# Twelve attention layers on one core: score matmuls that wait for one bank each, restacking by row slot, and softmax denominators spread by a VectorE shuffle

## What is computed

```python
for i in range(6):                                    # D=128, 16 heads of 8 channels, DFF=512
    xn = adaln(x, noise_emb, n1_w[i], n1_b[i])        # layernorm, gain and shift from the condition
    q, k, v = split(xn @ qkv_w[i].T); q, k = rope(q), rope(k)
    x = x + softmax(q k / sqrt(8)) v @ so_w[i].T      # over 512 tokens
    xn = adaln(x, noise_emb, n2_w[i], n2_b[i])
    q = rope(xn @ cq_w[i].T); k = rope(context @ ck_w[i].T); v = context @ cv_w[i].T
    x = x + softmax(q k / sqrt(8)) v @ co_w[i].T      # over 154 context tokens
    xn = adaln(x, noise_emb, n3_w[i], n3_b[i])
    x = x + gelu(xn @ f1_w[i].T + f1_b[i]) @ f2_w[i].T + f2_b[i]
```

## Time and profile before

| | |
|---|---|
| median of 3 runs | 3327.22 us (3326.3 to 3336.64) |
| the profiled execution's own time | 3326.18 us |
| its span, first to last instruction | 3324.4 us |
| mean granted TensorE clock | 0.956 |
| PE busy | 2934.0 us (88%) |
| DVE busy | 2097.4 us (63%) |
| ACT busy | 1917.6 us (58%) |
| POOL busy | 823.6 us (25%) |
| first stack, from about 720 to 1943 us | 6 layers |
| second stack, from about 2000 to 3213 us | 6 layers |

### The profile page before, as it was taken

One profiled execution on the slowest core, in us unless ns is written; L12 is line 12 of the kernel. 1 busy time (PEld: TensorE's weight loads), 2 busy tenths in 40 slices (PEclk: granted clock), 3 DMA queues, 4 the chain that ended last, 5 costly groups with the idle time before them and its releaser, 6 DMA issues.

```text
span 3324.4 us, 44923 instructions
## 1 busy us (share of the span) xinstructions
PE 2934.0 (88%) x15735; PEld 1036.8 (31%) x15735; DVE 2097.4 (63%) x3631; ACT 1917.6 (58%) x2693; POOL 823.6 (25%) x1327
## 2 busy tenths in 40 slices
PE   7998999977989899898989856989989898998978
PEld 2473333321222323222232222232322223232226
DVE  4316776637668495766848465848576684857634
ACT  5433333334758576675857642857667585766742
POOL 0002455431222222222222201222222222222211
PEclk9999999987999999999999976999999899999999
DMA  1101000001111111111111100111111111111130
GB/s 45 58 1 26 1 1 1 1 16 37 32 34 39 40 34 37 41 38 32 41 41 29 42 13 20 40 40 29 40 45 36 32 41 40 29 38 45 38 128 7
DMA packets 125514, 110.11 MB, mean 33 GB/s; under 512 B 49982, under 2 KB 116076, under 8 KB 125292
## 3 DMA queue, kind: packets, MB, share of 16 engines
q1 hardware_dynamic: 114924, 97.80, 9.9%
q10 hardware_dynamic: 10368, 9.44, 0.9%
HBM read 41.96 MB, written 0.52 MB: 13 GB/s over the span
## 4 chain that ended last, share of the span: by engine, by line
PE 65%; DVE 18%; ACT 6%; issue 4%; POOL 3%; SPq 1%; ACTq 1%; DMA 1%; DVEq 0%; POOLq 0%
PE ps L515 12%; DVE arena L798 7%; PE ps L460 7%; PE ps L489 3%; PE ps L588 3%; PE ps L631 3%; PE ps L646 3%; PE ps L532 3%; PE ps L574 2%; PE ps L1492 2%; PE ps L523 2%; PE ps L1480 2%; PE ps L544 2%; PE ps L563 2%; ACT arena L671 2%
## 5 line engine op out<-in xcount | busy, mean ns | idle before, releaser
L671 ACT ACTIVATE arena<-ps 128x1024 f32<-128x1024 f32 x960 | 934.4, 1022 | 245.9 <-PE ps L489 235.5
L798 DVE TENSOR_REDUCE arena<-ps 128x1 f32<-128x512 f32 x1536 | 964.6, 683 | 118.9 <-PE ps L460 109.7
L515 PE MATMUL ps<-arena 128*32 128x512 f32 x3840 | 504.2, 606 | 2.2 <-ACT arena L690 1.2
L460 PE MATMUL ps<-arena 49*128 49x512 bf16 x1536 | 311.6, 402 | 149.0 <-DVE arena L798 107.7
L800 DVE TENSOR_REDUCE arena<-ps 128x3 f32<-128x462 f32 (+1 forms) x576 | 305.2, 579 | 137.6 <-PE ps L467 116.3
L489 PE MATMUL ps<-arena 52*128 52x512 bf16 x1920 | 342.9, 385 | 29.5 <-ACT arena L671 8.6
L880 POOL TENSOR_TENSOR arena<-arena,zeros 128x16 bf16<-128x16 f32 x192 | 42.3, 220 | 1085.7 <-DVE arena L798 711.6
L460 PEld LDWEIGHTS ps<-arena 49*128 49x128 bf16 x1536 | 75.0, 93 | 542.9 <-DVE arena L798 470.8
L890 POOL TENSOR_TENSOR arena<-arena 128x512 f32<-128x512 f32 x96 | 122.1, 1272 | 387.4 <-ACT arena L703 384.1
L1552 ACT ACTIVATE arena<-ps 128x1024 f32<-128x1024 f32 x96 | 98.1, 1022 | 165.9 <-DVE ps L1639 128.9
L355 PE MATMUL ps<-consts 128*128 128x512 f32 x336 | 163.4, 612 | 23.7 <-DVE arena L2076 23.7
(11 more groups left out here) (383 smaller groups left out, 4366.5 us busy)
## 6 DMA issues: line engine op xcount, KB each, us to landing
arena<-arena SPq DMA_DIRECT2D x720, 64.0 KB
arena<-we_dram SPq DMA_DIRECT2D x24, 578.5 KB, 7.5
arena<-arena ACTq DMA_DIRECT2D x144, 64.0 KB
w<-weights_dram SPq DMA_DIRECT2D x26, 320.0 KB, 3.2
w<-weights_dram SPq DMA_DIRECT2D x13, 512.0 KB, 4.2
arena<-arena SPq DMA_DIRECT2D x384, 6.0 KB
arena<-arena SPq DMA_DIRECT2D x288, 19.2 KB
w<-weights_dram SPq DMA_DIRECT2D x39, 128.0 KB, 2.2
```

The lines of the kernel that those rows point to most:

```text
L460: pe.matmul(s_bank(slot + r), qst[b][rows, idx, P * qt:P * (qt + 1)], kst[b][rows, idx, :], start=True, stop=True).then_inc(s_full, 1)
L515: mm = pe.matmul(bank(7)[32 * j:32 * j + 32, :], v, prob[:, slot, j, :], start=(g % 2 == 0 and kt == 0), stop=(a == 0 and g % 2 == 1 and k ...
L671: act.activation(prob[:, chunk_no(b, a, g, kt) % NPROB, 2 * p:2 * p + 2, :], e_bank(slot).rearrange("p (j n) -> p j n", j=2), ACT.Exp, sca ...
L798: op = ve.tensor_reduce(nmax[:, g % 2, r, n:n + 1], s_bank(slot + r), AX.X, ALU.max, negate=True)
```

## The change

Four things change together.

1. **Score waits.** In self attention each of the two score matmuls waits for its own bank, not the first for both. Some waits of DVE and ACT are put in another sequence within one instruction.
2. **Restacking by row slot.** An `st` item is now one slot (two DMAs, four for the context's k) and waits for the part which that slot holds. The number of DMAs stays 96 a layer. Nine items, 18 DMAs a layer, are issued by ACT, where it was two items with 12 DMAs.
3. **Denominators.** The matmul in `sel` is gone, with `selector2` and what made it. DVE instead runs a `stream_shuffle` within each 32 partitions from `osb` to `rlog`, 8 a layer of 128 x 512 fp32; ACT's logarithm reads that from SBUF, and `sel` no longer uses a PSUM slot. The shuffle waits for `evac` and for the `inv` before it.
4. **Order.** `PLACES` has new numbers for all items (392 places, since `st` has more items), and `FILL` has 11 useless matmuls a layer in other places.

```diff
-PER_LAYER = 371
+PER_LAYER = 392
...
-        def restack(eng, b, u, part):
-            for slot in slots_of(u, part):
-                for r in range(2):
-                    rows = slice(64 * r + slot, 64 * r + ROW_MASK, PARTS)
...
+        def restack(eng, b, u, slot):
+            part = part_in(u, slot)
+            for r in range(2):
+                rows = slice(64 * r + slot, 64 * r + ROW_MASK, PARTS)
...
-        ACT_STACKS = (("st", 0, 1, 0), ("st", 1, 2, 0))
+        ACT_STACKS = (("st", 0, 1, 0), ("st", 0, 1, 1), ("st", 0, 2, 4), ("st", 1, 0, 2), ("st", 1, 0, 3),
+                      ("st", 1, 0, 5), ("st", 1, 1, 0), ("st", 1, 2, 4), ("st", 1, 2, 5))
...
-        FILL = {("out", 0, 1): 3, ("out", 1, 1): 2, ("f1", 0, 0): 1, ("score", 1, 1, 0, 0): 2, ("center", 0, 2): 1}
+        FILL = {('center', 0, 2): 1, ('out', 0, 1): 2, ('out', 1, 1): 3, ('score', 0, 0, 0, 4): 1, ('score',
+                0, 0, 1, 2): 1, ('score', 1, 1, 0, 0): 2, ('var', 0, 2): 1}
...
             def score(it):
...
-                pe.wait_ge(s_free, z.room("s", it, 2))
                 if a == 0:
                     idx, qt = 2 * g + n // 4, n % 4
                     for r in range(2):
                         rows = slice(64 * r, 64 * r + K_SCORE)
+                        pe.wait_ge(s_free, z.room("s", it, 1) if r == 0 else floor0(at - 1))
                         pe.matmul(s_bank(slot + r), qst[b][rows, idx, P * qt:P * (qt + 1)], kst[b][rows, idx, :],
                                  start=True, stop=True).then_inc(s_full, 1)
                     return
+                pe.wait_ge(s_free, z.room("s", it, 2))
...
-            def sel(it):
-                _, b, a, e = it
-                slot, at = z.use("e", it)
-                pe.wait_ge(v_free, z.after("evac", ("evac", b, a, e), it))
-                pe.wait_ge(e_free, z.room("e", it, 1))
-                pe.matmul(e_bank(slot)[:, 0:S], selector2[:, :], osb[:, e, :], start=True, stop=True)\
-                  .then_inc(e_full, 1)
...
             def sel(it):
                 _, b, a, e = it
-                slot, at = z.use("e", it)
-                act.wait_ge(e_full, at + 1)
-                act.wait_ge(den_inv, z.ahead("inv", it))
-                act.activation(rlog, e_bank(slot)[:, 0:S], ACT.Ln).then_inc(e_free, 1)
+                act.wait_ge(den_spread, z.after("sel", it))
+                act.activation(rlog, rlog, ACT.Ln).then_inc(den_log, 1)
...
+            def sel(it):
+                _, b, a, e = it
+                ve.wait_ge(v_free, z.after("evac", ("evac", b, a, e), it))
+                ve.wait_ge(den_inv, z.ahead("inv", it))
+                ve.stream_shuffle(rlog, osb[:, e, :], [HD] * 16 + [16 + HD] * 16).then_inc(den_spread, 1)
```

More of the change, by code:

```diff
@@ L190 @@
 COUNTED = ["s", "e", "group", "hi", "c", "q0", "k0", "q1", "k1", "row0", "row1", "chunk", "tail", "ktail", "split", "pv", "pvt",
-           "evac", "inv", "sq", "rstd", "ln", "scaled", "rope", "first", "bias", "n0", "n1", "n2", "self", "cross", "sout", "cout", "ffn"]
+           "evac", "sel", "inv", "sq", "rstd", "ln", "scaled", "rope", "first", "bias", "n0", "n1", "n2", "self", "cross", "sout", "cout", "ffn"]
 class Stretch:
@@ L579, in proj @@
                 slot, at = z.use("s", it)
+                if it in FILL:
+                    pe.wait_ge(s_free, z.room("s", it, 1))
+                    fill(it, s_bank(slot))
                 if u == 3:
@@ L648, in f2 @@
                 mm.then_inc(s_full, 1)
-            does = {"score": score, "turn": turn, "exp": exp, "tail": tail, "pv": pv, "pvt": pvt, "sel": sel, "out": out,
+            does = {"score": score, "turn": turn, "exp": exp, "tail": tail, "pv": pv, "pvt": pvt, "out": out,
                     "center": center_h, "var": var, "proj": proj, "vals": vals, "gain": gain, "f1": f1, "f2": f2}
```

176 lines of the change are left out of this document (88 added, 88 removed), and 3 rows, old and new, of the table PLACES.

## The result

The changed kernel takes 3405.23 us (median of 4 runs, 3396.24 to 3419.17), the kernel before 3327.35 beside it: a ratio of 1.0247, 95% interval 1.0208 to 1.0285. It is slower by some 82 us by the ratio and 78 by the medians; 3254 was forecast, with a range up to 3330. The profiled execution has a span of 3402.6 us.

A forecast was written before the change was run, and what follows sets the result against it. PE was taken as the bound, alone in the context stretch, with DVE narrowly ahead in the score stretch. From 3326 us, -47 - 14 + 17 - 12 - 16 = -72 gave 3254, range 3185 to 3330.

The forecast's parts named there:

- The cover of the useless matmuls: Two more a layer, 0.94 us each, hidden by waits before out and for DVE at score start; uncovered, +23 us.
- Selector matmuls: Eight a layer leave PE; four, between sequence 1's scores and f2, count at 0.98 us over 12 layers: -47 us.
- Rival B: All eight selector matmuls of a layer count and no clock fall is left: 3190 us; chance 0.17.
- The seam: Chain from ACT's last copy to out shrinks from 4.6 to 3.4 us a layer: -14 us, bound 0.
- Shuffles: Eight a layer on DVE at 0.69 us; only the two in DVE's score stretch cost: +17 us, bounds 0 to 22.
- rival E: DVE, working in order, stands some 2.6 us at shuffles waiting for ACT's evac, holding up PE: 3348 us; chance 0.13.
- the prediction's own signs: DVE's idle time before shuffles released by ACT's copy: below 1 us a layer refutes E; E decides for slower from 6.8.
- the third of E's places: Shuffle ahead of the next layer's k rope; the other two stand among sequence 1's maxima; 2.6 us wait at each.
- Split score waits: First matmul of a score pair starts with one bank free, cutting PE's waits for DVE's maxima: 1 us a layer, -12.
- Clock falls: Shorter score-start waits regain half of the 33 us lost where PE's granted clock falls: -16 us, bounds -33 to +13.
- rival C: More short PE gaps make the clock fall in every layer, 3.8 us each: 3283 us; chance 0.13.
- Edits at nothing: Added useless matmuls (uncovered +23 us) and ACT's 18 DMA issues a layer, not 12 (uncovered +52), priced at 0.

The follow-up runs named there:

- a_sel: Changed kernel with its third part undone: selector matmul on PE and ACT's logarithm from PSUM again, all else kept; 3498.69 us, ratio 1.0504 to the kernel before.
- b_shuf: Kernel before with the selector matmul replaced by the shuffle alone, in the old order with the old useless matmuls; 3425.89 us, ratio 1.0316.
- b_mix: Kernel before with split score waits and the shuffle, into the reciprocals' buffer, only for self attention of sequence 1; 3314.28 us, ratio 0.9976.
- b_mix4: Kernel before with split score waits and the shuffle, into the reciprocals' buffer, for self attention of sequences 1 and 0; 3353.43 us, ratio 1.0091.
- b_rinv_split: Kernel before with the shuffle into the two reciprocal buffers, some sel and inv places earlier, and split score waits; 3379.03 us, ratio 1.0151.
- b_late2: Kernel before with items behind out of sequence 1 placed later among the scores, second half of f1 ahead of sequence 0's first Exp; 3381.77 us, ratio 1.0180.
- a_fill: Changed kernel with the useless matmuls of the kernel before (9 a layer), nothing else undone; 3370.91 us, ratio 1.0125 to the kernel before.
- a_act: Changed kernel with the old useless matmuls and restacking DMAs shared between SP and ACT as in the kernel before (12 a layer on ACT); 3504.47 us, ratio 1.0534.
- a_ffn0: Changed kernel with the old useless matmuls and sequence 1's first two context score items behind sequence 0's first f1; 3407.31 us, ratio 1.0257.
- b_split: Kernel before with the split score wait alone; 3316.59 us, ratio 0.9976.
- a_hold: Changed kernel with the old useless matmuls, two more ahead of sequence 1's out, one each at its third layer norm's mean and variance; 3375.42 us, ratio 1.0153.
- a_joint: Changed kernel with its first part undone: both score matmuls of a pair wait together for two banks; 3415.04 us, ratio 1.0281 to the kernel before.
- b_rinv: Kernel before with the shuffle writing into the two reciprocal buffers, sel and inv of e = 0 earlier in three of four attentions; 3368.47 us, ratio 1.0119.

## Why the prediction was wrong

The forecast was 72 us faster, and the kernel is some 80 us slower. Two steps failed: the clock term, at -16 with +13 as its worst, and the order, which had no term at all. The cover of the useless matmuls, put at nothing, comes third.

*Selector matmuls (-47, bounds 0 to -94).* Matmul against shuffle together make 86 us by a_sel, where the sum has -47 + 17 and a part of the seam's -14; from the kernel before the same exchange costs 105 (b_shuf), so its sign hangs on the order. The reason given, that PE decides the context stretch and so each matmul counts, holds for two of the four: with the selector back, the fourth window takes 16.7 us and not 14.6 (means), all of 2 x 0.98. For the two between the outs of self attention b_mix refutes it: 2 x 0.98 us gone there gave 0.3. A stage in which PE is busy 95% still had something else that ended last. Rival B had the size, and not its sum.

*The seam (-14).* The chain was right, and the stage won more. ACT's last copy to `out` is this chain in the changed kernel:

```profile
2466.75 0.60 ACT L693 ACTIVATE arena<-ps 128x512 f32<-128x512 f32 x1 [1.75 <-PE ps L530]
2467.39 0.01 DVE L816 LOAD_MASK_SELECT lg<-arena  x1 [4.01 <-ACT arena L693]
...
2470.83 1.98 PE L543 MATMUL ps<-arena,w 128*128 128x512 f32 x4 [1.38 <-POOL arena L898]
```

3.48 us, where 3.4 was forecast; the whole stage from `f2` to `out` won 3.4 a layer as a mean, 41 us.

*Shuffles (+17), and rival E.* The duration was right:

```profile
L816 DVE STREAM_SHUFFLE lg<-arena x96: 716/726/744, 835.4 to 3270.6; 128x512 f32<-128x512 f32 x96
its engine sat idle before it (us, times) until:
  ACT arena L693: 95.3, 24
```

726 ns against 692 taken. The Trainium skill, in "VectorE: DVE Perf Modes", section "The perf-mode tier table (the rule you actually need)", led to an estimate of 0.80 us; the measured 0.726 decides. In DVE's stretch a shuffle cost twice its length (b_mix4). E's wait is there, 7.9 us a layer, and by the prediction's own signs (refuted below 1, decisive from 6.8) E would have been read as shown. But it stands at the two shuffles ahead of `out`, 3.0 us of it at the third of E's places, the one ahead of the rope, in a stage that became shorter; none stands at the shuffles among the maxima. So E had the sign of the change, and what the windows lost lies elsewhere.

*Split score waits (-12).* About right in the old order (8 us, at the edge of what can be told) and 11 us in the new, inside the interval; beside the two-buffer shuffle they went with 11 us more (b_rinv_split). The step "0.2 us, half of 0.39" was wrong: a score alone takes 0.39, since the pair's two lie over each other.

*Clock falls (-16) and rival C.* Here the sum failed. I took half of 33 us as regained, and capped the worst case at one fall of 3.8 us a layer (+13). The profiles have 211 us more at the low clock. What that costs, the kernel before says: its window of 54.2 us at 0.91 stood 2 x 0.09 x 54.2 = 9.8 us at the low level and took 3.8 longer, 0.39 for each, so 211 us come to 82. That is an estimate, and it is as large as the whole loss. The falls came in every layer, as C said, but longer: 17 us at 1.2 GHz, where it was 10, and 9.5 us more from `out` to `f2` as a mean, some of it work moved into that window; the shortest layer of the change took 198.6 us. The Trainium skill's rule on C, in "TensorE: Matmul & The Clock Gate", section "A second HAM failure mode: psum-queue depth-cycling", that short idling of PE between groups of matmuls in cycled banks makes the clock swing, agrees with b_late2 in kind: the fall follows a row of short matmuls into cycled banks. It does not say where: the score stretch cycles the same banks and held 1.00.

*Edits at nothing.* The new useless matmuls cost 34 us by a_fill (41 by the ratios), more than the +23 named; those at score items wait for banks and run at 2.07 us where the clock is down. The step that failed is the cover: PE's wait for DVE ends at the moment when the useless matmul may start. The restacking was put at nothing too: PE now waits 31.1 us for its DMAs at the context scores, where it was 2.7. That ACT's issues cost nothing was not tried by itself. It is also not six that move: twelve DMAs a layer go from SP to ACT and six from ACT to SP, and undoing that in the new order (a_act) costs 0.041.

*What had no term.* The order itself. The part on the change had its rows: the mean matmul behind three score items, not one. The prediction priced instructions added and removed, and no instruction that merely stood elsewhere. By ratios, and taken off the changed kernel in this sequence, its 82 us are the shuffle's -86, about +41 of useless matmuls, and +127 of the other order with restacking by slot and split waits; in another sequence the shares differ, as the shuffle's does. No run has the restacking by slot alone. b_late2 shows 60 us for a score start of that kind in the kernel before. The rest of the 127 is not settled: the longer stretch from `out` to `f2` of sequence 0 comes with 2.1 us of waiting for a restacking DMA and an `f1` at half clock, and a_ffn0 only changed these for other waits. Nor was the clock varied by itself: no run had the new order at full clock. The estimate above would make the clock the larger part; how much of those 127 us it is, and how much waiting, stays open. No version tried is clearly faster than the kernel before; b_split and b_mix, both 0.9976, are within the 0.3% that can be told.

## What to carry to other kernels

When a change comes with a new order, price the order first: for the engine with the most work, list every row of short, dependent instructions that goes at another engine's pace, and what long work stands between them before and after. A matmul without use is free only where its own wait ends before that of the work behind it; if both wait for the same buffer it is a delay, and even where it holds the clock it can cost what the clock gives (a_hold). The same exchange of instructions won 86 us in one order and lost 105 in the other, so an edit tried in one order says little of the next. And taking work from the busiest engine of a stage is worth its length only if a trace shows which wait ends last there; two matmuls less were worth 0.3 us of 1.96.

## What the runs showed of the hardware

Two bf16 matmuls of 49 rows, on rows 0 to 48 and 64 to 112, lie over each other when they are issued together: 0.39 us for the pair, and 0.39 for one alone. Separating them by a wait cost PE 88 us of busy time in the old order (b_split) and 107 in the new (the change against a_joint); neither kernel became slower by it, but beside the two-buffer shuffle it went with 11 us more. A DVE shuffle of 128 x 512 fp32 takes 0.73 us, with 0.01 for its mask. A restacking DMA holds the queue of the engine that issues it for 0.7 us: in b_rinv ACT's copy starts 0.1 us behind six of them (4.2 us). Which queue issues them weighed more than any single edit of the compute here: twelve a layer moved from ACT to SP and six the other way cost 0.041 of the time (a_fill 1.0125, a_act 1.0534), in an order made for the other sharing.
